# A transformer layer on one core: other places in the hand-written order for 30 MLP turns, the query and key products, and the work that goes with them

## The reference, cut to what matters

```python
# x: (16, 1024, 256), 16 heads of 16, F = 1024
xn = _layernorm(x)
Q, K, V = xn @ Wq.T + bq, xn @ Wk.T + bk, xn @ Wv.T + bv      # split in 16 heads
Q, K = _rope(Q, pos), _rope(K, pos)
scores = where(causal, einsum('bhqd,bhkd->bhqk', Q, K) / sqrt(16), -1e9)
attn = einsum('bhqk,bhkd->bhqd', softmax(scores), V)           # heads put together again
h = square(relu(einsum('bsd,fd->bsf', xn, W_fc)))
y = einsum('bsf,df->bsd', h, W_proj)
# five steps of: reset = mem > 1; mem = 0.9 * mem + y - reset; spike = mem > 1
out = x + (attn @ Wo.T + bo) + spikes_summed / 5
```

## Time and profile before

| | |
|---|---|
| median of 3 runs | 2168.79 us (2166.99 to 2172.21) |
| the profiled execution's own time | 2166.99 us |
| its span, first to last instruction | 2165.3 us |
| PE busy | 2088.6 us, 96% of the span |
| ACT, DVE, POOL busy | 1444.7, 1385.3, 1111.0 us |
| mean granted clock of TensorE | 0.993 |
| 16 DMA engines, queue of SP | 47.6% of their time, 296.10 MB |

### The profile page before, as it was taken

One profiled execution on the slowest core, in us unless ns is written; L12 is line 12 of the kernel. 1 busy time (PEld: TensorE's weight loads), 2 busy tenths in 40 slices (PEclk: granted clock), 3 DMA queues, 4 the chain that ended last, 5 costly groups with the idle time before them and its releaser, 6 DMA issues.

```text
span 2165.3 us, 67675 instructions
## 1 busy us (share of the span) xinstructions
PE 2088.6 (96%) x25492; PEld 1510.5 (70%) x25492; DVE 1385.3 (64%) x2139; ACT 1444.7 (67%) x1676; POOL 1111.0 (51%) x1072
## 2 busy tenths in 40 slices
PE   5999999999999999999999999999999999999995
PEld 4677676777767677676777767677676777767663
DVE  7576585766758566585666758566585666757443
ACT  3666667676676767667667676767667667676662
POOL 5464463645546455464645546455463645646341
PEclk9999999999999999999999999999999999999998
DMA  5353636445364553635445364553635445364442
GB/s 200 120 165 95 186 103 170 128 120 184 93 178 119 138 168 95 193 106 158 140 120 180 93 179 120 135 172 95 195 106 155 143 120 178 91 175 126 113 115 71
DMA packets 169866, 299.97 MB, mean 139 GB/s; under 512 B 25104, under 2 KB 114960, under 8 KB 157200
## 3 DMA queue, kind: packets, MB, share of 16 engines
q1 hardware_dynamic: 169616, 296.10, 47.6%
HBM read 174.89 MB, written 103.28 MB: 128 GB/s over the span
## 4 chain that ended last, share of the span: by engine, by line
PE 81%; ACT 4%; DMA 4%; DVE 4%; issue 3%; SPq 2%; POOL 1%; ACTq 0%; DVEq 0%; POOLq 0%
PE pair L1530 22%; PE pair L1327 21%; PE pair L1513 12%; PE pair L1336 9%; PE pair L1305 7%; PE pair L1253 5%; PE pair L1319 4%; ACT probs L813 3%; SPq L441 2%; DMA recip_rows<-recip_dram 2%; DMA qk_dram<-rot_b 1%; PE pair L1271 1%; PE pair L1468 1%; DVE xn L951 1%; DVE rot_b L1004 0%
## 5 line engine op out<-in xcount | busy, mean ns | idle before, releaser
L813 ACT ACTIVATE probs<-pair 128x1024 f32<-128x1024 f32 x1152 | 1139.7, 1029 | 503.8 <-PE pair L1513 502.0
L688 POOL TENSOR_TENSOR h_lo<-h_sq,h_hi 128x512 fp32r<-128x512 f32 x256 | 409.9, 1601 | 478.0 <-DVE h_hi L1072 477.6
L1336 PE MATMUL pair<-wproj_hi,h_hi 64*128 64x256 f32 x2048 | 590.1, 288 | 0.0
L1336 PE MATMUL pair<-wproj_hi,h_lo 64*128 64x256 f32 x2048 | 572.3, 279 | 0.0
L1336 PE MATMUL pair<-wproj_lo,h_hi 64*128 64x256 f32 x2048 | 571.6, 279 | 0.0
L1327 PE MATMUL pair<-xT_hi,wfc_hi 64*128 64x256 f32 x2048 | 551.0, 288 | 6.4 <-DVE fin L1019 2.5
L696 POOL TENSOR_SCALAR_AFFINE_SELECT probs<-probs 128x512 f32<-128x512 f32 x512 | 376.4, 753 | 341.9 <-ACT probs L813 341.9
L1530 PE MATMUL pair<-probs,v_sb 128*17 128x512 f32 (+3 forms) x6144 | 545.3, 488 | 0.9 <-ACT probs L813 0.9
L1327 PE MATMUL pair<-xT_lo,wfc_hi 64*128 64x256 f32 x2048 | 536.0, 280 | 0.0
L1327 PE MATMUL pair<-xT_hi,wfc_lo 64*128 64x256 f32 x2048 | 535.2, 279 | 0.0
L1513 PE MATMUL pair<-q_ring,k_ring 64*128 64x512 f32 (+3 forms) x3072 | 442.4, 355 | 19.6 <-ACT probs L813 14.1
(11 more groups left out here) (113 smaller groups left out, 2901.8 us busy)
## 6 DMA issues: line engine op xcount, KB each, us to landing
q_ring<-qk_dram SPq DMA_DIRECT2D x384, 128.0 KB
k_ring<-qk_dram SPq DMA_DIRECT2D x384, 128.0 KB
qk_dram<-planes SPq DMA_DIRECT2D x64, 512.0 KB, 2.8
qk_dram<-rot_b SPq DMA_DIRECT2D x62, 512.0 KB, 3.8
xn<-in_x SPq DMA_DIRECT2D x16, 1024.0 KB, 5.6
rs<-in_x SPq DMA_DIRECT2D x64, 256.0 KB, 2.8
acc_dram<-rs SPq DMA_DIRECT2D x64, 256.0 KB, 2.2
attn<-numer SPq DMA_DIRECT2D x256, 64.0 KB, 2.4
```

Of the source, the lines that this page charges most:

```text
L688: pool.tensor_tensor(h_lo[i % HB][:, :], h_sq[i % HB][:, :], h_hi[i % HB][:, :].bitcast(F32), ALU.subtract).then_inc(h_lo_done, 1)
L813: act.activation(probs[BUFFER[n]][:, 2 * pr:2 * pr + 2, :], pair[m % NSLOT][:, :, :], ACT.Exp, scale=SCALE).then_inc(exp_done, 1)
L1336: return pe.matmul(proj_bank[:, t * D:(t + 1) * D], h[rows, a * T2 + t * P:a * T2 + (t + 1) * P], w[rows, f, :], start=i % ITEMS_OF_GROUP ...
```

## The change

It changes only entries of the tables, so which place each piece of work has in the order of its engine. No instruction is added or removed.

- `VALUES_AT`: the second turn of value product 0 moves from (0, 2) to (0, 3), ahead of the first turn of product 1.
- `QK_AT`: the second turn of product 0, with its rotation, moves from (3, 0) to (3, 1), behind one more score product; the first turn of product 2 from (4, 4) to (4, 3).
- `SUM_QK_AT`, `PLANE_AT`, `SQUARE_AT` and `LOW_QK_AT` get the same places in each step.
- `MLP_AT`: 11 of the 30 turns move by one or two places; turns 5 and 6, 11 and 12, 19 and 20, 27 and 28 now stand together.
- `RELU_AT` follows `MLP_AT`: each item's relu, square, copy and low part stand at the place of the turn that ends its expansion. Only item 1 has its own place, (7, 3).
- `Y_CARRIED_AT` moves from (1, 4) to (1, 0), and so ahead of the reciprocal at (1, 3).
- Spikes, bias additions, statistics and normalising get more regular places.

```diff
-VALUES_AT = {(0, 0): ((0, 0),), (0, 2): ((0, 1),), (0, 3): ((1, 0),), (1, 0): ((1, 1),), (1, 3): ((2, 0),),
-             (1, 4): ((2, 1),)}
+VALUES_AT = {(0, 0): ((0, 0),), (0, 3): ((0, 1), (1, 0)), (1, 0): ((1, 1),), (1, 3): ((2, 0),), (1, 4): ((2, 1),)}
-QK_AT = {(2, 4): (0, 0), (3, 0): (0, 1), (3, 3): (1, 0), (4, 0): (1, 1), (4, 4): (2, 0), (5, 0): (2, 1),
+QK_AT = {(2, 4): (0, 0), (3, 1): (0, 1), (3, 3): (1, 0), (4, 0): (1, 1), (4, 3): (2, 0), (5, 0): (2, 1),
-SUM_QK_AT = {(2, 4): 0, (4, 2): 1, (5, 2): 2, (6, 1): 3}
-PLANE_AT = {(3, 4): 0, (5, 0): 1, (6, 0): 2, (7, 1): 3}
-SQUARE_AT = {(4, 2): 0, (5, 0): 1, (6, 0): 2, (7, 0): 3}
-LOW_QK_AT = {(7, 3): 3}
+SUM_QK_AT = {(3, 2): 0, (4, 2): 1, (5, 2): 2, (6, 2): 3}
+PLANE_AT = {(3, 4): 0, (4, 4): 1, (5, 4): 2, (6, 4): 3}
+SQUARE_AT = {(4, 2): 0, (5, 2): 1, (6, 2): 2, (7, 2): 3}
+LOW_QK_AT = {(7, 2): 3}
-MLP_AT = {(6, 4): (0,), (7, 0): (1,), (7, 4): (2,), (8, 2): (3, 4), (8, 4): (5,), (9, 2): (6,), (9, 4): (7, 8),
-          (10, 1): (9,), (10, 4): (10,), (11, 0): (11,), (11, 1): (12,), (11, 3): (13, 14), (12, 0): (15,),
-          (12, 3): (16,), (13, 0): (17,), (13, 3): (18,), (14, 0): (19,), (14, 1): (20,), (14, 4): (21, 22),
-          (15, 2): (23,), (15, 3): (24,), (16, 0): (25,), (16, 3): (26,), (17, 0): (27,), (17, 1): (28,),
-          (17, 3): (29,)}
+MLP_AT = {(6, 3): (0,), (7, 0): (1,), (7, 4): (2,), (8, 2): (3, 4), (8, 4): (5, 6), (9, 3): (7, 8), (10, 0): (9,),
+          (10, 3): (10,), (11, 0): (11, 12), (11, 3): (13, 14), (12, 0): (15,), (12, 3): (16,), (13, 0): (17,),
+          (13, 3): (18,), (14, 0): (19, 20), (14, 3): (21, 22), (15, 0): (23,), (15, 3): (24,),
+          (16, 0): (25,), (16, 3): (26,), (17, 0): (27, 28), (17, 3): (29,)}
-Y_AT = {(10, 1): 0, (13, 1): 1, (16, 0): 2}
+Y_AT = {(10, 0): 0, (13, 0): 1, (16, 0): 2}
-Y_CARRIED_AT = (1, 4)
+Y_CARRIED_AT = (1, 0)
-RELU_AT = {(7, 0): (0,), (7, 2): (1,), (8, 2): (2,), (8, 4): (3,), (9, 4): (4,), (10, 2): (5,), (11, 0): (6,),
-           (11, 3): (7,), (12, 3): (8,), (13, 1): (9,), (14, 0): (10,), (14, 4): (11,), (15, 2): (12,),
-           (16, 0): (13,), (17, 2): (14,), (17, 4): (15,)}
+RELU_AT = {**expanded_at(MLP_AT, NFC), (7, 0): (0,), (7, 3): (1,)}
...
-BIAS_HERE_AT = {(7, 3): (0,), (10, 4): (1,)}
-BIAS_NEXT_AT = {(13, 4): (0,), (16, 1): (1,)}
-STATS_AT = {(10, 1): (0, 1), (10, 2): (2,), (10, 3): (3,), (11, 1): range(4, 7), (11, 4): (7,)}
+BIAS_HERE_AT, BIAS_NEXT_AT = {(8, 2): (0,), (10, 2): (1,)}, {(14, 2): (0,), (15, 4): (1,)}
+STATS_AT = {(10, 3): range(0, 4), (11, 4): range(4, 8)}
...
-XN_AT = {(16, 2): range(0, 4), (17, 4): range(4, 8)}
+XN_AT = {(16, 4): range(0, 4), (17, 4): range(4, 8)}
```

More of the change, by code:

```diff
@@ L176 @@
 INVERT_LAST, DIVIDE_LAST, INVERT_AT, DIVIDE_AT = (1, 3), (3, 0), (11, 0), (14, 0)
-SPIKES_HERE = {(8, 3): (0, 0), (9, 0): (0, 1), (9, 1): (0, 2), (9, 2): (0, 3), (9, 3): (0, 4), (10, 0): (0, 5),
-               (10, 3): (1, 0), (10, 4): (1, 1), (11, 0): (1, 2), (11, 3): (1, 3), (11, 4): (1, 4), (12, 0): (1, 5)}
-SPIKES_NEXT = {(13, 2): (0, 0), (14, 1): (0, 1), (14, 2): (0, 2), (14, 3): (0, 3), (14, 4): (0, 4), (15, 0): (0, 5),
-               (15, 1): (1, 0), (15, 2): (1, 1), (16, 1): (1, 2), (16, 3): (1, 3), (17, 0): (1, 4), (17, 4): (1, 5)}
+SPIKES_HERE = {(8, 3): (0, 0), (8, 4): (0, 1), (9, 1): (0, 2), (9, 2): (0, 3), (9, 3): (0, 4), (9, 4): (0, 5),
+               (10, 2): (1, 0), (10, 3): (1, 1), (10, 4): (1, 2), (11, 1): (1, 3), (11, 2): (1, 4), (11, 3): (1, 5)}
+SPIKES_NEXT = {(14, 1): (0, 0), (14, 2): (0, 1), (14, 3): (0, 2), (14, 4): (0, 3), (15, 1): (0, 4), (15, 2): (0, 5),
+               (15, 3): (1, 0), (15, 4): (1, 1), (16, 1): (1, 2), (16, 2): (1, 3), (16, 3): (1, 4), (17, 1): (1, 5)}
 SPIKES_FINAL = {(16, 0): 0, (17, 0): 1}
-BIAS_HERE_AT = {(7, 3): (0,), (10, 4): (1,)}
-BIAS_NEXT_AT = {(13, 4): (0,), (16, 1): (1,)}
-STATS_AT = {(10, 1): (0, 1), (10, 2): (2,), (10, 3): (3,), (11, 1): range(4, 7), (11, 4): (7,)}
+BIAS_HERE_AT, BIAS_NEXT_AT = {(8, 2): (0,), (10, 2): (1,)}, {(14, 2): (0,), (15, 4): (1,)}
+STATS_AT = {(10, 3): range(0, 4), (11, 4): range(4, 8)}
 VAR_AT, ROOT_AT = (11, 4), (12, 0)
-XN_AT = {(16, 2): range(0, 4), (17, 4): range(4, 8)}
+XN_AT = {(16, 4): range(0, 4), (17, 4): range(4, 8)}
 def spike_thresholds():
```

## The result

The changed kernel takes 2202.7 us in the median (2200.13 to 2207.49, 4 runs), the kernel before 2168.63 us beside it (2166.99 to 2172.21, 4 runs). The ratio is 1.0155, 95% interval 1.0136 to 1.0175: 34 us slower. The sign is the one forecast, the size is three times the forecast of 11 us, and it lies above the range. The profiled execution took 2198.70 us, 31.7 us more than the one of before.

A forecast was written before the change was run, and what follows sets the result against it. PE's work was taken as the bound, so only its waits could change. Terms of +1.05 us on a quick round became +0.8 for 14 rounds, +0.3 for round 0: 2178.5 us profiled, 2180 us median; 8-in-10 range 2165 to 2193 us.

The forecast's parts named there:

- Copy of y ahead of the reciprocal: Steps 1 to 3: reciprocal ends 1.2 us later, its rows land later, division and product 1 wait: +0.9 us a round.
- Steps 4 to 7: Swaps of product 2's first turn with a score product, and of sums, copies and squares, cost nothing.
- Relu of item 1: Step 7: between two exponentials it delays a score product, +0.4 us in a quick round; late transfer stops mattering, -0.2 mean.
- turn 6: Steps 8 and 9: right behind turn 5, it waits for the low part of item 2 on POOL, +0.25 us.
- score products of step 9: Two score products there no longer wait for ACT: -0.4 us a round.
- rival 2: Faster: ACT runs far enough ahead that no score product waits, step 7 or 9 to 11; -0.4 a round, 2163 us, 12%.
- Steps 9 to 11: Hand-written order with ACT's exponentials and relus: short score product waits remain, -0.1 us, between -0.9 and +0.3.
- Steps 12 to 17 and the values in step 0 come out the same: No gain or loss claimed in the round's last steps or at the value products of step 0.
- Round 0: First round: has all the terms but the division, about +0.3 us.
- rival 1: Not slower: landing before the division isn't tied to the reciprocal; 0.0 a round, 2169 us; 18% together with rival 4.
- rival 4: The order hides everything, a swap among overlapping waits: 2169 us; one case with rival 1, together 18%.
- Rival 3: Slower still: POOL's low parts reach the pairs of turns late, two collisions with DVE a round, +1 us more; 2194 us, 15%.

The follow-up runs named there:

- three chosen ones: Kernel before with turn 6 at (9, 0), relu of item 1 at (7, 4), last division at (3, 1), behind the rotation: 2157.14 us, ratio 0.9932.

## Why the prediction was right in sign and wrong in size

- **What bounds the kernel:** right. PE's work didn't change, only its waits, and the clock is where it was.
- **Copy of y ahead of the reciprocal, +0.9 with the later turn of product 0:** the mechanism was right in every link, and the entry alone costs 0.4 to 0.6 us a round on the kernel before. In the kernel after the two together measure +0.50 at product 1 (25.23 to 25.73) and +0.57 at step 4: 0.17 for the turn, 0.33 for the copy. The term was sized against a quick round (25.10), and against that it is 0.63: the forecast had the division start 21.8 us into the round, and in this execution it starts at 21.58. Another 0.13 was already being lost in the mean, to late landings. The division takes 1.41 us in the mean, near the 1.45 assumed; it is lengthened in 11 of the 14 rounds, not in every one (5 of 14 before).
- **Steps 4 to 7 at nothing:** they gave back 0.2 us.
- **Relu of item 1, +0.4 less 0.2; turn 6, +0.25; score products of step 9, -0.4:** measured +0.17, +0.31 and -0.39, and the first of them alone, on the kernel before, +0.18. Right, and so is rival 2's defeat: the score product at (8, 1) waits.
- **Steps 9 to 11, -0.1:** wrong, +0.42. This is the first step that failed. The order had been written out for ACT alone, "with exponentials of 0.92 us pace and relus of 0.5 us". What decides is the queue of DVE: the copy of y behind an addition that POOL's low part stretches from 0.69 to 1.67 us. Moving four additions one place, this one among them, removed it (steps 10 and 11 took 14.33 us and then 13.88, 13.91 before).
- **"Steps 12 to 17 and the values in step 0 come out the same":** wrong, and the dearest sentence of the prediction, 0.97 of the missing 1.08 us a round. The pairs of turns 11 and 12, 19 and 20, 27 and 28 did have the time that was claimed (turn 12 takes 1.44 us, 1.60 before). But the masks, which nobody had followed, went behind the low part of item 11 on POOL, and that low part came 0.5 us later beside the bias additions. Moving the additions back took 0.5 of the wait away, through the square and the rounded copy on DVE; putting the relu back behind the masks took the wait for masks away and gave 0.63 to turn 24. What stays in either case is read from the trace and had no run of its own: turns 21 and 22 now stand ahead of the score product at (14, 4), which starts 111.4 instead of 107.6 us into the round. The masks need its exponential, so that they and the low part become ready within 2 us of each other, on an engine that takes 1.7 to 2.1 us for each, and the sums follow 1.4 us sooner. Moving these turns back wasn't tried.
- **Round 0, +0.3:** +4.5. 1.5 of it are the two failed steps; 0.9 is the turn of values taken out of (0, 2), and 1.5 come in step 7: 0.9 the low part of product 3 colliding with a low part on POOL, the rest a later relu. These are read from the trace and had no run of their own; what is left are smaller waits in steps 3 to 6.
- **The rivals:** rivals 1, 2 and 4 fell. Rival 3 was nearest: it had the engine (POOL), the kind of loss (its low parts, and collisions with DVE of half a microsecond and more) and 2194 us, but placed it at the pairs of turns, and got 15%.

The sum by the measured terms, 14 x 1.88 + 4.7 + 0.7, is what the profile shows; the forecast had 14 x 0.8 + 0.3. Two readings of the prediction are wrong without touching its sum: the waits that it lists add up to 2.3 us and not 2.6, and the one slice with a lower clock is the last of the 40, not the first.

## What to carry to other kernels

When an order is changed on engines that each work strictly in turn, write out every queue whose output the bound engine reads, not just the busiest one; here POOL at 51% and DVE at 64% took back more than ACT at 67%. A producer that is moved earlier can be the loss by itself, since it gets in front of something more urgent or in the way of another engine's instruction, so list what stood behind the new place and what it releases. And rather than swapping many entries at once, try few: three chosen ones gave 14 us together where the whole change lost 34.

## What the runs showed of the hardware

- A collision of DVE and POOL costs the later instruction. The addition of 128 x 512 on DVE takes 0.69 us when it starts 0.17 us ahead of POOL's low part, which then takes 1.68. Started 0.55 us behind, it takes 1.67, and ends 0.55 us after POOL is done. In round 0 the low part, 0.17 us behind a DVE instruction of 1.22, took 2.17 instead of 1.27. The Trainium skill, page "SBUF — State Buffer", section "Who interferes with whom", states this as a lock on a shared port on which the later one blocks; the three pairs agree, and by it the loss at step 10 could have been foreseen. The later one ends 0.11 to 0.15 us sooner in them than a full wait and its own length would give.
- The collisions form chains. At step 10 the low part starts 0.17 us behind a DVE instruction in either order and takes 1.67 or 1.68 us; what differs is whether another such instruction stands behind that one on DVE, which then loses 0.98 us and delays the copy behind it. In step 15 two bias additions on POOL cost PE 0.5 us, since DVE's rounded copy takes 0.84 us beside them and 0.43 without.
- The landing of the reciprocal's rows, 512 KB written from a small source, is not a fixed time: 7.6 to 9.4 us from the issue in one execution of the kernel before, 8.2 to 9.7 in one with the relu of item 11 moved, with the same loads around it. Product 1 started between 25.73 and 26.26 us into the round in five executions that issue these transfers alike. That moves a kernel whose division waits for it by up to 7 us from one execution to the next, as much as two of the effects studied; in the version where the division stands behind the rotation it moves nothing.
